# Moving the weight-chunk loads of the ternary quantizer from SyncE's DMA queue to GpSimd's, and to both in turn at the end

## What is computed

```python
def _quantize(w):
    gamma = jnp.mean(jnp.abs(w))
    return jnp.clip(jnp.round(w / (gamma + EPS)), -1.0, 1.0)

def _bitlinear(x, w):
    return jnp.matmul(x, _quantize(w).T)

x = x + _layernorm(attn(_layernorm(x), Wq, Wk, Wv, Wo))
h = sigmoid(_bitlinear(ln, w1)) * _bitlinear(ln, w2)     # ln = _layernorm(x)
x = x + _layernorm(_bitlinear(h, w3))
```

## Time and profile before

| | us |
|---|---|
| median of 3 runs | 11663.99 |
| lowest and highest run | 11506.55, 11735.09 |
| the profiled execution, its own time | 11508.99 |
| its span (core 1, the slowest) | 11507.4 |
| spans of the 8 cores | 11381.3 to 11507.4 |
| TensorE busy | 6831.4 (59%) |
| VectorE busy | 2899.7 (25%) |
| ScalarE busy | 2598.9 (23%) |
| GpSimd busy | 303.2 (3%) |

### The profile page before, as it was taken

One profiled execution on the slowest core, in us unless ns is written; L12 is line 12 of the kernel. 1 busy time (PEld: TensorE's weight loads), 2 busy tenths in 40 slices (PEclk: granted clock), 3 DMA queues, 4 the chain that ended last, 5 costly groups with the idle time before them and its releaser, 6 DMA issues.

```text
span 11507.4 us, 111527 instructions; the slowest of 8 cores (11381.3 to 11507.4 us)
## 1 busy us (share of the span) xinstructions
PE 6831.4 (59%) x31808; PEld 3085.0 (27%) x31808; DVE 2899.7 (25%) x5841; ACT 2598.9 (23%) x5541; POOL 303.2 (3%) x500
## 2 busy tenths in 40 slices
PE   0535773222221135799759981667755699839983
PEld 0222332111100012343224330334322244314431
DVE  1322664333332323100010003334433200020001
ACT  1132664333332212100000001006632100010001
POOL 0000000000001100000000000000000000000000
PEclk9867776555555567899979995777777899868997
DMA  6334224333332232222232212220022222121212
GB/s 110 100 110 124 78 69 145 110 111 110 110 94 86 72 82 76 94 77 63 60 108 77 64 57 91 56 55 2 1 64 79 90 77 66 56 104 62 74 54 81
DMA packets 719188, 921.26 MB, mean 80 GB/s; under 512 B 329600, under 2 KB 510336, under 8 KB 697472
## 3 DMA queue, kind: packets, MB, share of 16 engines
q1 hardware_dynamic: 668384, 638.33, 19.0%
q0 software_dynamic: 50208, 275.81, 7.6%
HBM read 715.69 MB, written 174.06 MB: 77 GB/s over the span
## 4 chain that ended last, share of the span: by engine, by line
PE 43%; DMA 17%; DVE 14%; SPq 9%; issue 8%; ACT 8%; DVEq 1%; ACTq 0%; POOL 0%; POOLq 0%
PE PS L1005 11%; PE PS L1012 11%; SPq L128 9%; PE PS L1049 7%; DMA ARENA<-w3T_h 6%; PE PS L929 4%; DMA w3T_h<-ARENA 4%; PE PS L852 3%; PE PS L497 3%; PE PS L815 2%; DVE ARENA L344 2%; DVE PS L824 2%; ACT ARENA L829 2%; DVE ARENA L370 2%; DVE ARENA L507 1%
## 5 line engine op out<-in xcount | busy, mean ns | idle before, releaser
L1005 PE MATMUL PS<-ARENA 128*128 128x512 bf16 x5632 | 1719.2, 388 | 410.1 <-DMA ARENA<-w2T_h 410.1
L1012 PE MATMUL PS<-ARENA 128*128 128x512 bf16 x5632 | 1719.0, 388 | 0.0
L497 PE MATMUL PS<-ARENA 128*128 128x128 bf16 x2112 | 512.4, 264 | 1687.6 <-ACT ARENA L504 1359.2
L1049 PE MATMUL PS<-ARENA 128*128 128x512 bf16 x5632 | 1357.8, 389 | 242.1 <-DMA ARENA<-w3T_h 192.5
L344 DVE TENSOR_REDUCE ARENA<-ARENA 128x1 f32<-128x2048 f32 (+1 forms) x128 | 292.6, 2286 | 2924.4 <-ACT ARENA L1059 1614.1
L1005 PEld LDWEIGHTS PS<-ARENA 128*128 128x128 bf16 x5632 | 560.0, 99 | 1105.2 <-issue 533.8
L713 PE MATMUL PS<-ARENA 128*128 128x512 bf16 x2560 | 645.6, 419 | 337.9 <-DMA ARENA<-wq_bf 284.2
L829 ACT ACTIVATE ARENA<-PS 128x512 bf16<-128x512 f32 x1280 | 764.4, 597 | 277.3 <-DVE PS L824 200.2
L1025 DVE TENSOR_TENSOR ARENA<-ARENA,PS 128x1024 bf16<-128x1024 f32 x176 | 214.9, 1221 | 2420.2 <-ACT ARENA L1021 2420.2
L1049 PEld LDWEIGHTS PS<-ARENA 128*128 128x128 bf16 x5632 | 519.6, 99 | 1080.2 <-issue 639.5
L815 PE MATMUL PS<-ARENA 128*128 128x512 bf16 x1280 | 580.0, 488 | 320.2 <-ACT ARENA L829 270.6
(11 more groups left out here) (78 smaller groups left out, 4788.4 us busy)
## 6 DMA issues: line engine op xcount, KB each, us to landing
ARENA<-w SPq DMA_DIRECT2D x1056, 256.0 KB, 3.0
ARENA<-w1T_h SPq DMA_DIRECT2D x176, 512.0 KB, 3.3
ARENA<-w2T_h SPq DMA_DIRECT2D x176, 512.0 KB, 3.3
ARENA<-w3T_h SPq DMA_DIRECT2D x704, 128.0 KB, 2.0
ARENA<-x POOLq DMA_DIRECT2D x64, 1024.0 KB, 7.2
y_h<-ARENA POOLq DMA_DIRECT2D x32, 1024.0 KB, 4.2
ARENA<-y_h POOLq DMA_DIRECT2D x32, 1024.0 KB, 5.6
out<-ARENA POOLq DMA_DIRECT2D x32, 1024.0 KB, 4.2
```

What stands on the lines that cost most here:

```text
L497: e.transpose(ps, src, ident[:]), inc="T")
L1005: e.matmul(px1[wi][:, seg * 512:(seg + 1) * 512], w1sl[:, wi, dc, :], ln2Th[:, dc, seg * 512:(seg + 1) * 512], start=(dc == 0), stop=(dc = ...
L1012: "tensor", lambda e, dc=dc, seg=seg, wi=wi: e.matmul(px2[wi][:, seg * 512:(seg + 1) * 512], w2sl[:, wi, dc, :], ln2Th[:, dc, seg * 512:(s ...
L1049: "tensor", lambda e, i=i, hc=hc, wi=wi: e.matmul(pfs[i], hidT[:, hc, i * P:(i + 1) * P], w3sl[:, wi, :], start=(hc == 0), stop=(hc == c.H ...
```

## The change

Both load functions choose the queue. While `eng_pref` isn't "ALT" (LN, QKV and attention of the first sequence) every chunk load is issued by GpSimd. In the tail the loads go by the buffer's number: odd ones to SyncE, on a channel of its own ("g1s" for "g1"), even ones to GpSimd; of 17 buffers that is 8 and 9. The wait for the buffer moves with the load. The channel is handed on with the buffer, so that the computation waits for the right semaphore. Where attention starts, GpSimd and not SyncE waits for TensorE before the 12 loads into the new buffers. The quantizer's function is changed in the same way as the one for gamma, which is shown:

```diff
             gb, ch = G3[bid]
-            b.wait("sync", pst["gt"].get(bid))
-            b.dma("sync", gb[:],
+            ie = ("sync" if bid % 2 else "gpsimd") \
+                if pst.get("eng_pref") == "ALT" else "gpsimd"
+            if ie == "sync":
+                ch = ch + "s"
+            b.wait(ie, pst["gt"].get(bid))
+            b.dma(ie, gb[:],
                   w_in.rearrange("a bq -> (a bq)").rearrange(
                       "(n p x) -> n p x", p=P, x=c.GCH)[r0], ch=ch)
-            pst["pend"].append(bid)
+            pst["pend"].append((bid, ch))
...
     def gamma_comp(col):
         def fn():
-            bid = pst["pend"].popleft()
-            gb, ch = G3[bid]
+            bid, ch = pst["pend"].popleft()
+            gb, _ = G3[bid]
...
         if bb == 0 and not pst.get("grown") and NEXTRA > 0:
             pst["grown"] = True
-            b.wait("sync", ("T", b.sem["T"][1]))
+            b.wait("gpsimd", ("T", b.sem["T"][1]))
```

More of the change, by code:

```diff
@@ L533, in fn @@
                 srcv = w3v[hc][:, half * nb:(half + 1) * nb, :]
-                b.dma("sync", gb[:].rearrange("p (a j) -> p a j", j=P),
+                b.dma(ie, gb[:].rearrange("p (a j) -> p a j", j=P),
                       srcv, ch=ch)
             else:
-                b.dma("sync", gb[:],
+                b.dma(ie, gb[:],
                       w_in[hc * P:(hc + 1) * P,
```

## The result

| | before | after |
|---|---|---|
| median of 20 runs, us | 11639.29 | 11413.67 |
| lowest, highest, us | 11414.54, 11858.2 | 11290.33, 11603.01 |
| after / before | | 0.9879, 95% interval 0.9835 to 0.9924 |

The change makes the kernel 1.2% faster, between 0.8 and 1.7%, about 140 us. The forecast was 11440 us and 140 us less. That fits, but part of it is luck, as the stages show.

A forecast was written before the change was run, and what follows sets the result against it. SyncE's list was taken to bound QKV. Terms -97 - 49 + 6 + 8 + 4 + 3 - 15 gave -140 us; from a middle of 11586 that is 11446, predicted as 11440, range 11310 to 11600.

The forecast's parts named there:

- SyncE's list bounds QKV: QKV of sequence 0: the stage goes at the speed of SyncE's list, where transposing DMAs stand behind chunk loads.
- Q and K, -97 + 6 us: Q and K groups: 25.37 us each falls to 20.53, 97 us in both halves; 6 us given back beside chunk loads.
- I stay near the lower end: 3 us per half: Q and K: chunk loads beside transposing DMAs cost 3 us per half, between bounds of nothing and 18 us.
- number 1: Rival, QKV and start: chunk transfers give the gain back, no change, 11509; it or anything up to the forecast 0.14.
- SyncE waits more than it issues: SyncE's queue: 54.7 us of buffer waits outweigh issue, against the issue-only rule's saving of 55 us and time of 11454.
- V, -49 + 8 us: V groups: stretches of 84.8 and 82.2 us fall to 59, gaining 49; traffic beside V tiles gives 8 back.
- The start, +4 us: Before the first tile of x: four chunk loads after the last cast cost 4 us, bounds 0 and 16.
- The tail, +3 - 15 us: Tail: thresholds' tiny DMAs behind chunk loads, +3 us; less disturbed w3 stores, -15 us, bounds 0 and 70 over 44 slabs.
- VectorE isn't held up: Tail, VectorE's line 577: GpSimd's 326 added calls cost 1 us, left out; 80 us if each took 0.45.
- Number 3: Rival, tail: GpSimd becomes the bound between slab stores; about 11980 us at 8 us per load; chance 0.06.
- Number 2: Rival, more than 2% faster: w3's stores get their full 70 us and V tiles go below 3.1 us; 11290; chance 0.12.
- Number 4: Rival, V tiles: loads still bind through GpSimd, 4 us per tile instead of 3.15; 11396; chance 0.68 together with the forecast.

The follow-up runs named there:

- the small loads: Changed kernel with the QKV stage's gamma loads cut from 512 to 16 columns: Q and K 209.0 and 208.6 us, V 75.0 and 73.8 us.
- the split alone: Kernel before with only the tail's loads split between SyncE and GpSimd: w3 787.7 us instead of 801.3, 16 us less up to the output projection.

## Why the prediction was right, and where it was off

- **SyncE's list bounds QKV**: right. The move for QKV and attention alone brings 97 us; with ScalarE's queue in place of GpSimd's the Q and K stretch is the same to about 1 us. Both are shown by single edits.
- **The 11440 us**: 140 us less than a guessed middle of 11586 us. From the median before over 20 runs, 11639.29, the same gain would have given 11499; that 11440 lies 26 us from the measured 11413.67 is luck. "A fast execution should show 11370" came from a profiled execution of 11509 us, while before goes down to 11414.54; the changed kernel goes down to 11290.33.
- **Q and K, -97 + 6 us**: measured -64. Two costs were wrong, and a smaller error stands beside them. The floor of 20.53 us per group was read on core 1, whose stretch in sequence 1 is 205.3 us; four of the cores have 205 to 206 there, the other four about 209: 4 us in both halves. And the step "I stay near the lower end: 3 us per half" failed: traffic costs 12 us per half, of which 10 are shown by the small loads, 18 us more than forecast in both halves. I had inferred the 3 us from groups that begin behind five loads in flight; a burst of 60 keeps the engines full for 80 us, and landing goes to 5.5 us, over the 5.1 us that I had named as the point from which it counts. The bound of 18 us held. "Groups above 23 us beside chunk loads" stood in the prediction as a sign of being wrong (number 1), and on core 4 five of the twenty groups are above it, all beside the burst. The last 5 of the 27 us missing are the stretch before, taken as ten times 25.37 us from core 1's half 1; as medians over the cores the halves take 252.4 and 250.5.
- **"SyncE waits more than it issues"**: wrong for Q and K. The 54.7 us of waits in the earlier trace rows lie over the whole window; 14.3 of them fall on its nine Q and K periods, and the larger part on the loads between and behind the V groups. With six buffers a group's loads cost 2.86 us without any wait. The Trainium skill's rule ("DMA: Bandwidth & Descriptors", section "Issuing engines are not separate DMA queues") that only issue time is saved is nearer than I took it to be: 29 us of issue and 11 of waits per half, less the traffic. With 0.48 us instead of 0.33 per load it would have given 120 x 0.48, 58 us, for Q and K. That 64 were measured is no proof of it: leaving SyncE's list gave back some 88 us over the floor in both halves, and traffic took 24 of them.
- **V, -49 + 8 us**: measured -34. ScalarE's pace was taken as the next bound, 3.15 us per tile. On core 4 it was (618.72 - 567.02) / 15 = 3.45, and between GpSimd's last load and the next tile of x, behind the barrier, 4.9 us passed:

```profile
567.02 0.37 ACT L781 CAST ARENA<-PS 128x256 bf16<-128x256 f32 x1 [167.40 <-PE PS L770]
...
618.72 0.38 ACT L781 CAST ARENA<-PS 128x256 bf16<-128x256 f32 x1
...
621.14 0.63 ACT L443 ACTIVATE ARENA<-ARENA 128x512 bf16<-128x512 f32 x1 [1.23 <-DMA ARENA<-w]
```

```profile
627.93 0.53 POOL L128 DMA_DIRECT2D ARENA<-x  x1 [4.92 <-issue]
```

  The small loads show that the missing time is the chunks' transfer: with it gone the pace is 2.90 us, which is ScalarE's own. The 3.15 us were not: the stretch of the earlier trace rows that they were read from already held 2.1 us of waits for chunks.
- **The start, +4 us**: measured +2.5, within its bounds of 0 and 16. The reason given for the 4 doesn't hold: four chunks are 1 MB, as much as the tile, and at the tile's rate they would take all of its 12.41 us and not a third.
- **Attention, 0**: 724.6 both times. The lead of 16 chunks hides the loads on either queue.
- **The tail, +3 - 15 us**: the thresholds, forecast at +3, measured -2.6, and the split alone shows the same sign (-3.3): this term was wrong in sign, and no run shows why. The gamma rest, forecast at 0, measured +2.3. w3, forecast at -15, measured -11.8: the stores' chain became shorter as forecast, and the split alone shows it again (-13.6). On core 4 the 132 gaps between the stores of a slab fall from 319.6 to 294.0 us in sum. That this comes from loads no longer flying beside the stores was argued from the order of the list and not tested by itself.
- **VectorE isn't held up**: right as far as line 577 shows it, which has the same two cases as in the earlier trace rows. What VectorE's second comparison waited for in the changed kernel, core 4:

```profile
  DVE ARENA L582: 0.9, 2
```

- **The rivals.** Number 1 was a part of the truth: a quarter of what leaving SyncE's list brings in Q and K is taken back by transfers, not all of it. Number 3 was far off: two loads of w3 take 1.5 us of a gap of 8.6. Number 2 named the right place, w3's stores, but the 70 us bound it set is that of disturbed landings; the larger sum in the chain itself, 178 us (789.5 - 612.0), needs another edit. Number 4 is what happened in the V tiles, at 3.45 instead of 4 us.

The sum of the stages is 104 us and not 140. The runs show about 140, with the 104 inside their interval; by the stages the forecast of the change was 35% too high, and that it meets the ratio of the runs is luck as far as the stages can tell.

## What to carry to other kernels

A transfer that must wait for a buffer belongs in a list in which nothing urgent stands behind it; which engine's list that is, GpSimd's or ScalarE's, mattered by about 1 us in Q and K and by 4 in V, and the plain issue of many small DMAs can cost as much as their waits. Freed loads run ahead as fast as their buffers allow, so ask what the burst flies beside: if the neighbour keeps only four transfers in flight, its margin is a number to compare with its landing time under load. And read a floor over all the cores before it goes into a sum.

## What the runs showed of the hardware

- A chunk load costs SyncE 0.48 us in its list when nothing makes it wait (6 in 2.86 us), though its issue shows as 0.33 us in the earlier trace rows. On GpSimd the issue shows as 0.54 us, and as 0.76 for a load of w3 in four pieces.
- Transposing DMAs land in 2.4 us alone and in 5.5 us beside a queue that keeps the DMA engines full; 60 loads of 8 KB in place of 256 KB leave them at 2.5.
- The rate of issuing them differs between cores for the same code: 204 to 207 us for 160 on cores 1, 3, 5 and 7, 208 to 211 on cores 0, 2, 4 and 6, in every profiled execution (half 1 of sequence 1).
- Four stores of 128 KB in a row from GpSimd take it 2.29 us and land together soon enough to save 4.0 us per slab over four that wait for each other.
